# PSUM's eight banks dealt out anew in a fused attention and feed-forward kernel: four for the scores of the exponentials, two for the maxima

## The chip, the cores and the metric

The kernel runs on one core of one Trainium2 chip. The metric is the device time of one execution in microseconds (us). The names of the engines in the rows are those of the profile: PE is TensorE's matmul, PEld its weight load, DVE is VectorE, ACT is ScalarE, POOL is GpSimd, SP is SyncE, which here issues all DMAs.

## The reference

For x of 1024 rows by 512 columns, in fp32:

```
q = x Wq (32 heads of 16)      k, v = x Wkv (8 groups of 16, each shared by 4 heads)
ctx = softmax(causal(q k^T) / 4) v
x1  = layernorm(x + ctx Wo + bo)
out = layernorm(x1 + x1 W^T + bias + LoRA(x1))
```

LoRA(x1) is a low-rank product of 8 adapters of rank 16; the kernel adds it into W beforehand.

## The kernel before, in words

**Units and cycles.** The queries are cut into two halves of 512, and the heads into 8 groups of 4; a half and a group are a *unit* (`NU` = 16, units 8 to 15 are the second half). A unit's scores for the exponentials are worked off in *cycles* (`CYCLES`, 80 of them, numbered 0 to 79): a cycle is 256 of the unit's queries against two blocks of 128 keys. Each cycle has four *pieces* (three where it lies on the causal diagonal); a piece is one matmul of 128 keys by 512 columns (line 1401), and ScalarE turns it into probabilities with one exponential (line 881), 288 in all. Afterwards 16 small matmuls (line 1379, `accumulate`) multiply the cycle's probabilities by v into bank 6.

**Maxima.** The exponentials need each row's maximum beforehand, so each unit's scores are computed a second time, queries on the partitions, some three cycles ahead. This work is cut into 304 *chunks* of at most one PSUM bank (`CHUNKS`): `chunk_scores` on TensorE (line 1164, 1 to 4 matmuls per chunk) and `chunk_max` on VectorE (lines 937 and 944). Of unit 8 on a query block has chunks against the first half's keys (`own` false, one `TENSOR_REDUCE`, line 937) and chunks against its own half (a masked maximum per head, line 944, followed by a short read of the accumulator). A unit's maxima are then split into three bf16 parts by GpSimd (lines 673 to 677), turned by TensorE (line 1172), copied by ScalarE (line 759) and moved by SyncE (line 520) into rows of the unit's queries, so that the score matmul subtracts them.

**Fillers.** Besides, TensorE's order has *fillers*, at most one per cycle (`FILL`): the remaining projections (Q, VT, WE) in cycles 0 to 19, and for each of the first four output blocks the six steps T1a, T1b, T2, WO, T3, FF from cycle 24 on, at offsets 0, 2, 5, 7, 10, 13 in blocks of 14 cycles (24 to 37, 38 to 51, 52 to 65), closer together in the last. Q, WO and FF are long ones (12 matmuls, three after each of the four lots), the others short. The last four output blocks follow after the cycles.

**TensorE's order in a cycle.** It is written out by hand: for each of four lots, the lot's chunks (`chunks_of_cycle`, 0 to 2 chunks), then one piece, then a part of the filler; after the fourth, `accumulate` for the cycle before, then possibly a turn of maxima. Engines take their instructions strictly in this order; VectorE takes the chunks in the same order, with the filler's results between them at fixed places (after T1a or T1b a normalisation of the context at the next cycle's start; after WO and FF the residual there, and the moments after the first lot; after T2, T3 and the projections a subtraction after the first lot).

**Banks.** PSUM has eight banks. Bank 6 holds the products with v. `ST_BANKS` = 3 banks (3 to 5) are dealt in turn to the pieces: a piece waits until the exponential of the piece three before it is done (line 1400). `MAX_BANKS` = 3 banks (0 to 2) and bank 7 (`MISC`) are shared by chunks, fillers and turns. `place_banks` (line 221) deals them out before the program is built: each user takes the bank that has been in use longest, except that a bank given to a filler or a turn is held (`held`) until the end of the next cycle; late fillers, of the last unit's lead, take bank 7. What a chunk has to wait for is in `CHUNK_BEHIND`: the chunk that had its bank before (`was_read`, line 1139, waits until VectorE has read it), or a filler. In this text the *distance* of a chunk is by how many chunks it is behind the one that it waits for. From the 15th chunk on, the distance is 3 for 195 chunks, 4 for 48, 2 for 15; 32 wait for a filler or a turn. The 15 with distance 2 lie in cycles 11, 14, 38 and 52, where two banks are held at once.

```
was_read(CHUNK_BEHIND[n])
for k, j in enumerate(heads):
    last = nc.tensor.matmul(PS[:, CHUNK_BANK[n], k * width:(k + 1) * width], ...)
last.then_inc(max_scores, 1)
```

**Start and end.** The products ahead of the cycles use banks 3 to 6 in a ring of their own (`RING`, `job_bank`); the first 14 chunks lie there, in banks `n % MAX_BANKS`. `FIRST_BEHIND` (line 1347) says which of these products had banks 3 to 6 before the first pieces. From the piece `WIDE` (number 255, in cycle 71) on, when no chunk is left, the pieces rotate over all six banks 0 to 5, whatever the division is.

Of the kernel before, what the change touches and what calls it, by code (L numbers as in the profile page):

```python
# [19 lines left out]
def postln_kernel(nc, x, wq, wkv, wo, bo, lora_a, lora_b, w, bias, lora_w, xt, out):  # L20
# [39 lines left out]
    def key_blocks(cyc):  # L60
        p = CYCLES[cyc][2]
        return 2 * p, 2 * p + 1
# [5 lines left out]
    def pieces(cyc):  # L68

        first = [(0, range(0, 2), 0), (0, range(2, 4), 0)]  # L70
        return first + ([(1, range(0, 4), P)] if on_diagonal(cyc) else [(1, heads, 0) for _, heads, _ in first])
# [66 lines left out]
    def nth(job, kinds):  # L138

        return sum(1 for j in JOBS[:JOB[job] + 1] if j[0] in kinds)  # L140
# [74 lines left out]
        return [lot[len(lot) * q // 4:len(lot) * (q + 1) // 4] for q in range(4)]  # L215


    MAX_BANKS, ST_BANKS = 3, 3
    PV_BANK, MISC = 6, 7

    def place_banks():
# [66 lines left out]
    with ctx:  # L288
# [126 lines left out]
        def score_bank(e):  # L415

            return MAX_BANKS + e % ST_BANKS if e < WIDE else (e - WIDE) % (MAX_BANKS + ST_BANKS)
# [4 lines left out]
        def freed(job):  # L422

            kind, b, _ = job
            if kind == "rows":
                return nm_rows, b + 1
            if kind in ("T1a", "T1b"):
                return ctx_ready, 2 * b + (2 if kind == "T1b" else 1)
            if kind in ("T2", "WO", "T3", "FF"):
                return {"T2": ct_ready, "WO": y1_read, "T3": x1t_ready, "FF": y2_read}[kind], b + 1  # L430
            if kind in BY_ACT:
                return v_read, nth(job, BY_ACT)
            return job_freed, nth(job, DVE_KINDS)
# [704 lines left out]
        def _(pe):  # L1138
# [208 lines left out]
            FIRST_BEHIND = {3 + n % RING: JOBS[n] for n in range(NJOB_A - RING, NJOB_A)}  # L1347
# [37 lines left out]
            def piece_scores(cyc, k):  # L1385

                u, s, _ = CYCLES[cyc]
                i, heads, skip = pieces(cyc)[k]
                kb = key_blocks(cyc)[i]
                e = SCORE_BANKS[cyc] + k  # L1390
                if e < ST_BANKS:
                    pe.wait_ge(*freed(FIRST_BEHIND[score_bank(e)]))
                elif WIDE <= e < WIDE + MAX_BANKS:
                    pe.wait_ge(max_read, len(CHUNKS))
                elif e >= WIDE + MAX_BANKS + ST_BANKS:
                    pe.wait_ge(probs, e - MAX_BANKS - ST_BANKS + 1)
                elif e >= WIDE:
                    pe.wait_ge(probs, WIDE)
                elif e >= ST_BANKS:
                    pe.wait_ge(probs, e - ST_BANKS + 1)  # L1400
                nc.tensor.matmul(PS[:, score_bank(e), :], KS[0:NROW, u % G, kb * P:(kb + 1) * P],  # L1401
                                 QS[0:NROW, u % SLOTS, heads[0]:heads[-1] + 1, s * HQ + skip:(s + 1) * HQ],
                                 start=True, stop=True).then_inc(scores, 1)

            for cyc, (u, _, _) in enumerate(CYCLES):
                if cyc == 0:
                    rows_moved()
                elif cyc == FIRST[u]:
                    pe.wait_ge(nm_in, 16 * NPART * u)
                for j, lot in enumerate(chunks_of_cycle(cyc)):  # L1410
                    for n in lot:
                        chunk_scores(n)
                    if j < len(pieces(cyc)):
                        piece_scores(cyc, j)
                    if cyc == rows_cycle(1) + 1 and j == 0:
                        turn_maxima(1)
                    filler(cyc, j)
                if cyc:
                    accumulate(cyc - 1)
                if cyc in ROWS_AT and ROWS_AT[cyc] > 1:  # L1420
                    turn_maxima(ROWS_AT[cyc])
# [65 lines left out]
```

## Time and profile before

| what | value |
|---|---|
| median of 3 runs | 337.27 us (336.91 to 337.57) |
| the profiled execution | 337.42 us, its span 335.7 us |
| PE, matmul | 320.8 us busy, 2493 instructions |
| PEld, weight loads | 170.9 us |
| DVE | 256.7 us |
| ACT | 217.3 us |
| POOL | 137.7 us |
| granted TensorE clock | 0.997 of full speed |

The span is the time from the first to the last profiled instruction; 1.7 us of the execution lie around it. Times in the rows are from the span's start. Matmuls are pipelined: the time from one's start to its end includes the way through the array, and the next starts before that. How full TensorE is must therefore be read from start to start. The cycles begin at 34.9 us (cycle 0) and end at 301.9 us with the last `accumulate`; the chunks end with cycle 69, at 273 us.

### The profile page before, as it was taken

To read this page: it belongs to the slowest core of one execution; us is meant where nothing else is said; L and a number is where in the kernel's file an instruction comes from. 1 tells how busy PE (TensorE), PEld (TensorE's weight loads), DVE (VectorE), ACT (ScalarE), POOL (GpSimd) and SP (SyncE) were. 2 spreads that over 40 slices of the span, in tenths; PEclk is the share of its full clock that TensorE was granted. 3 is DMA by queue.
4 is the path that set the end of the run, shared out by engine and by line. 5 is a ranking of instruction groups with operands and counts; after the bars stand their busy time and mean duration, and the time that the engine had idled before them with its cause. 6 is when DMAs were issued, how large, how long until landed. Compare 5 with 4: busy or idle time off the path is not lost.

```text
span 335.7 us, 7267 instructions
## 1 busy us (share of the span) xinstructions
PE 320.8 (96%) x2493; PEld 170.9 (51%) x2493; DVE 256.7 (76%) x787; ACT 217.3 (65%) x420; POOL 137.7 (41%) x270
## 2 busy tenths in 40 slices
PE   8999989999999999999999999999999999999992
PEld 3766345455444344454544544544544444558882
DVE  3567968989789989888789889888886961047664
ACT  5563737665757786858667678488584786952431
POOL 8775215464347495347112132212141123331553
PEclk9999999999999999999999999999999999999998
DMA  7687499634235110010020100000000000000002
GB/s 238 251 163 177 127 151 299 204 112 144 63 113 160 49 51 0 3 47 4 8 72 3 49 3 3 0 31 3 3 0 3 32 2 1 2 33 1 2 31 94
DMA packets 15363, 22.96 MB, mean 68 GB/s; under 512 B 3232, under 2 KB 8512, under 8 KB 15328
## 3 DMA queue, kind: packets, MB, share of 16 engines
q1 hardware_dynamic: 15328, 22.51, 23.6%
q8 instruction: 20, 0.33, 0.4%
q14 instruction: 15, 0.12, 0.1%
HBM read 16.29 MB, written 6.03 MB: 66 GB/s over the span
## 4 chain that ended last, share of the span: by engine, by line
PE 74%; DVE 5%; DMA 5%; ACT 4%; issue 4%; POOL 3%; SPq 3%; POOLq 0%; DVEq 0%; ACTq 0%
PE PS L1379 18%; PE PS L1224 17%; PE PS L1164 15%; PE PS L1401 15%; ACT PB L881 3%; DMA scr_q<-parts 2%; PE PS L1305 2%; PE PS L1297 2%; DVE scrap L944 2%; DVE MX L937 2%; PE PS L1239 2%; DMA X<-in_L_attn_x_turned_dram 1%; SPq L498 1%; POOL parts L590 1%; SPq L510 1%
## 5 line engine op out<-in xcount | busy, mean ns | idle before, releaser
L881 ACT ACTIVATE PB<-PS 128x512 f32<-128x512 f32 x288 | 155.5, 604 | 57.9 <-PE PS L1401 56.8
L944 DVE CUSTOM_DVE_ANT_0 scrap<-PS,mask 128x128 bf16<-128x128 f32 (+3 forms) x256 | 111.6, 487 | 15.9 <-PE PS L1164 15.2
L1164 PE MATMUL PS<-KS,QS 96*128 96x512 bf16 (+3 forms) x384 | 108.0, 329 | 2.2 <-DVE MX L937 1.0
L1401 PE MATMUL PS<-QS,KS 99*128 99x512 bf16 x288 | 106.3, 382 | 1.4 <-DMA QS<-NMR 1.1
L937 DVE TENSOR_REDUCE MX<-PS 128x1 f32<-128x512 f32 x128 | 81.9, 684 | 12.6 <-PE PS L1164 11.9
L711 POOL TENSOR_SCALAR_AFFINE_SELECT PB<-PB 128x256 f32<-128x256 f32 (+1 forms) x96 | 46.0, 483 | 102.7 <-ACT PB L881 99.7
L1379 PE MATMUL PS<-PB,VX 128*32 128x256 f32 (+1 forms) x1280 | 78.8, 364 | 0.6 <-ACT PB L881 0.3
L1164 PEld LDWEIGHTS PS<-KS,QS 96*128 96x128 bf16 x384 | 32.9, 97 | 49.7 <-issue 13.3
L1379 PEld LDWEIGHTS PS<-PB,VX 128*32 128x32 f32 x1280 | 33.5, 109 | 40.4 <-issue 17.5
L1401 PEld LDWEIGHTS PS<-QS,KS 99*128 99x128 bf16 x288 | 27.5, 98 | 30.8 <-ACT PB L881 7.4
L1224 PE MATMUL PS<-XT,WQ 128*128 128x512 f32 x120 | 37.4, 434 | 0.4 <-ACT NMR L759 0.4
L1224 PE MATMUL PS<-XT 128*128 128x512 f32 x96 | 28.1, 427 | 0.6 <-DVE MX L937 0.6
L1224 PE MATMUL PS<-WQ,XT 128*128 128x512 f32 x96 | 28.3, 427 | 0.0
L1224 PEld LDWEIGHTS PS<-XT,WQ 128*128 128x128 f32 x120 | 22.0, 190 | 5.9 <-ACT NMR L759 1.3
L692 POOL TENSOR_SCALAR mv<-mv 128x1 f32<-128x1 f32 x15 | 3.4, 227 | 48.7 <-DVE mv L1029 48.6
L944 DVE DVE_READ_ACCUMULATOR2_ANT MX<- 128x1 f32 x256 | 21.2, 83 | 0.0
L1224 PEld LDWEIGHTS PS<-XT 128*128 128x128 f32 x96 | 17.9, 190 | 4.6 <-DVE MX L937 1.1
L1224 PEld LDWEIGHTS PS<-WQ,XT 128*128 128x128 f32 x96 | 17.9, 190 | 4.0
L785 ACT ACTIVATE RAW<-PS 128x256 f32<-128x256 f32 x32 | 12.4, 387 | 10.6 <-PE PS L1379 10.4
L803 ACT ACTIVATE TC<-RAW,shift,rstd 128x512 f32<-128x512 f32 x7 | 5.7, 817 | 13.4 <-POOL shift L694 13.4
L747 ACT ACTIVATE parts<-PS 128x512 bf16<-128x512 f32 x10 | 6.0, 597 | 12.9 <-PE PS L1224 10.2
L590 POOL TENSOR_TENSOR parts<-TC,parts 128x512 bf16<-128x512 f32 x8 | 9.4, 1179 | 6.4 <-DVE NMPS L967 3.3
(102 smaller groups left out, 276.3 us busy)
## 6 DMA issues: line engine op xcount, KB each, us to landing
scr_q<-parts SPq DMA_DIRECT2D x8, 384.0 KB, 4.2
QS<-scr_q SPq DMA_DIRECT2D x15, 192.0 KB, 3.0
X<-in_L_attn_x_turned_dram SPq DMA_DIRECT2D x8, 256.0 KB, 5.8
X<-in_L_attn_x_dram SPq DMA_DIRECT2D x8, 256.0 KB, 2.8
out_dram<-TC SPq DMA_DIRECT2D x8, 256.0 KB, 2.0
QS<-scr_q SPq DMA_DIRECT2D x15, 128.0 KB, 3.0
RAW<-in_L_attn_Wo_dram SPq DMA_DIRECT2D x2, 512.0 KB, 4.9
RAW<-in_L_ffn_W_dram SPq DMA_DIRECT2D x2, 512.0 KB, 4.1
```

The lines of the kernel that those rows point to most:

```text
L590: nc.gpsimd.tensor_tensor(parts[:, s, 2, :], rest[:, s, :], parts[:, s, 1, :], ALU.subtract)\
L711: nc.gpsimd.affine_select(out=blk, in_=blk, compare_op=ALU.is_ge, fill=0.0, base=0, pattern=[[0, len(heads)], [1, P]], channel_multiplier=-1)\
L785: nc.scalar.activation(RAW[:, u, cols], PS[:, PV_BANK, cols], ACT.Copy).then_inc(raw_out, 1)
L881: nc.scalar.activation(PB[:, cyc % NP_BUF, k, :], PS[:, score_bank(e), :], ACT.Exp, scale=SCALE)\
L937: nc.vector.tensor_reduce(part[:, j0:j1, 0:1], bank, AX, ALU.max).then_inc(max_read, 1)
L944: last = nc.vector.tensor_tensor_reduce(out=scrap[:, n % 2, (j - j0) * width:(j - j0 + 1) * width], in0=bank[:, j - j0, :], in1=mask[:, HT ...
L1164: last = nc.tensor.matmul(PS[:, CHUNK_BANK[n], k * width:(k + 1) * width], QS[0:ROWS, u % SLOTS, j, qb * P:(qb + 1) * P], KS[0:ROWS, g, k0 ...
L1224: last = nc.tensor.matmul(bank, lhs(a, c), rhs(b, c), start=(k == 0), stop=(k == len(terms) - 1))
L1239: last = nc.tensor.matmul(job_bank(n), WQ[:, a, c, col:col + P], XT[:, b, c, 0:HT], start=(c == k == 0), stop=(c == NC - 1 and k == 2))
L1297: last = nc.tensor.transpose(bank[:, g * P:(g + 1) * P], RAW[:, h * G + g0 + g, qb * P:(qb + 1) * P], ident[:, :])
L1379: last = nc.tensor.matmul(PS[32 * j:32 * j + 32, PV_BANK, s * HQ + skip:(s + 1) * HQ], VX[:, key_blocks(cyc)[i], u % G, :], PB[:, cyc % NP ...
L1401: nc.tensor.matmul(PS[:, score_bank(e), :], KS[0:NROW, u % G, kb * P:(kb + 1) * P], QS[0:NROW, u % SLOTS, heads[0]:heads[-1] + 1, s * HQ + ...
```

## The change

```diff
-    MAX_BANKS, ST_BANKS = 3, 3
+    MAX_BANKS, ST_BANKS = 2, 4
     PV_BANK, MISC = 6, 7
...
                 e = SCORE_BANKS[cyc] + k
                 if e < ST_BANKS:
-                    pe.wait_ge(*freed(FIRST_BEHIND[score_bank(e)]))
+                    if score_bank(e) in FIRST_BEHIND:
+                        pe.wait_ge(*freed(FIRST_BEHIND[score_bank(e)]))
                 elif WIDE <= e < WIDE + MAX_BANKS:
```

Banks 2 to 5 go to the pieces, in turn, and banks 0, 1 and 7 to chunks, fillers and turns. A piece now waits for the exponential of the piece four before it. The first piece goes to bank 2, which no product of the start had, so that it has nothing to wait for there. `place_banks` deals the chunks and fillers out again by its rule, with one bank less; the order of instructions on every engine stays as it is, and so does their number. Bank 2's last user before piece 0 is one of the first unit's direct query moves, for which the first chunk waits already.

## Rows read from the trace of the kernel before

**Rows 1.** The page: busy time of the engines, and the chain that ended last

```profile
PE 320.8 (96%) x2493; PEld 170.9 (51%) x2493; DVE 256.7 (76%) x787; ACT 217.3 (65%) x420; POOL 137.7 (41%) x270
...
PE 74%; DVE 5%; DMA 5%; ACT 4%; issue 4%; POOL 3%; SPq 3%; POOLq 0%; DVEq 0%; ACTq 0%
```

**Rows 2.** Stretches: length, busy of PE, PEld, DVE, ACT, POOL, clock, DMA, GB/s

```profile
50.00:123.00 73.00, 70.54 (x588) 34.78 (x590) 64.88 (x244) 51.27 (x109) 39.89 (x80) 1.00 0.43 133
123.00:169.00 46.00, 45.98 (x397) 22.39 (x393) 40.20 (x118) 32.36 (x63) 23.63 (x38) 1.00 0.10 26
274.00:302.00 28.00, 27.16 (x256) 13.87 (x257) 5.96 (x15) 21.29 (x43) 8.33 (x19) 1.00 0.03 11
```

**Rows 3.** Timeline of cycle 27: start, length, engine, line; four chunks, distance 3

```profile
133.08 0.39 PE L1164 MATMUL PS<-KS,QS 96*128 96x512 bf16 x1
...
133.50 0.69 DVE L944 CUSTOM_DVE_ANT_0 scrap<-PS,mask 128x512 bf16<-128x512 f32 x1
...
134.12 0.08 DVE L944 DVE_READ_ACCUMULATOR2_ANT MX<- 128x1 f32 x1
...
134.26 0.09 PEld L1164 LDWEIGHTS PS<-KS,QS 96*128 96x128 bf16 x1 [0.20 <-DVE MX L944]
134.40 0.38 PE L1164 MATMUL PS<-KS,QS 96*128 96x512 bf16 x1
...
134.73 0.08 DVE L944 DVE_READ_ACCUMULATOR2_ANT MX<- 128x1 f32 x1
...
134.92 0.86 PE L1379 MATMUL PS<-PB,VX 128*32 128x256 f32 x16
...
135.71 0.39 PE L1164 MATMUL PS<-KS,QS 96*128 96x512 bf16 x1
```

**Rows 4.** Stretches of cycles 38, 52 and 66: same work; columns as before

```profile
169.45:172.83 3.38, 3.04 (x32) 1.48 (x29) 3.21 (x8) 2.23 (x4) 1.07 (x3) 1.00 0.00 0
214.90:218.25 3.35, 3.03 (x32) 1.48 (x29) 3.18 (x8) 2.23 (x4) 1.07 (x3) 1.00 0.00 0
261.15:264.01 2.86, 2.86 (x32) 1.56 (x29) 2.72 (x7) 2.12 (x4) 1.07 (x3) 1.00 0.00 0
```

**Rows 5.** Timeline of cycle 38: its three chunks, the last at distance 2

```profile
170.30 0.38 PE L1164 MATMUL PS<-KS,QS 96*128 96x512 bf16 x1
...
170.53 1.85 DVE L937 TENSOR_REDUCE MX<-PS 128x1 f32<-128x512 f32 x3
...
171.24 0.39 PE L1164 MATMUL PS<-KS,QS 96*128 96x512 bf16 x1 [0.34 <-DVE MX L937]
```

**Rows 6.** Timeline of cycle 66: the same chunks, the last at distance 3

```profile
262.43 0.38 PE L1164 MATMUL PS<-KS,QS 96*128 96x512 bf16 x1
```

**Rows 7.** Timeline of cycle 29: first chunk's end on DVE, third chunk's start on PE

```profile
139.95 0.38 PE L1164 MATMUL PS<-KS,QS 96*128 96x512 bf16 x1
...
140.12 0.08 DVE L944 DVE_READ_ACCUMULATOR2_ANT MX<- 128x1 f32 x1
```

**Rows 8.** Timeline of cycle 36: fourth chunk's start on PE, second chunk's end on DVE

```profile
162.21 0.38 PE L1164 MATMUL PS<-KS,QS 96*128 96x512 bf16 x1
...
162.75 0.08 DVE L944 DVE_READ_ACCUMULATOR2_ANT MX<- 128x1 f32 x1
```

**Rows 9.** Timeline of cycle 11: two chunks in one lot, beside a long filler

```profile
79.69 0.50 PE L1164 MATMUL PS<-KS,QS 96*128 96x384 bf16 x2
...
80.25 0.55 DVE L944 CUSTOM_DVE_ANT_0 scrap<-PS,mask 128x384 bf16<-128x384 f32 x1
...
80.72 0.08 DVE L944 DVE_READ_ACCUMULATOR2_ANT MX<- 128x1 f32 x1
```

**Rows 10.** Waits of pieces' weight loads: us in total, times, longest

```profile
PEld PS L1401 <- ACT PB L881: 7.4, 21, 0.8
```

**Rows 11.** Timeline around 43 us: unit 1's maxima copied, and moved by SyncE

```profile
42.33 0.27 ACT L759 ACTIVATE NMR<-PS 48x128 bf16<-48x128 f32 x1
...
43.87 3.05 SPq L520 DMA_DIRECT2D QS<-NMR  x3
```

## The prediction

> **What bounds the kernel now.** I read the page's busy times and its chain first [rows 1]. VectorE is busy for 76% of the span and matmuls for 96%, but a matmul's row includes the way through the array, so that 96% may hide idle time. The chain that ended last runs over TensorE for 74% of the span. The stretches [rows 2] say where: from 123 to 169 us, matmuls cover 45.98 of 46.00 us, while VectorE has 40.20 and ScalarE 32.36.
>
> How full TensorE is shows start to start in one cycle. Cycle 27 [rows 3] has four chunks of one bank, four pieces and no filler. Its first chunk starts at 133.08, its fourth (after three chunks and three pieces) at 134.40: six matmuls in 1.32 us, 0.22 us each. The fourth chunk and the fourth piece take 0.44 more, to 134.84, and the 16 small matmuls start at 134.92; the next cycle starts at 135.71. Of 2.63 us, 0.08 are not a matmul's own time. The stretches of cycles look like this nearly everywhere from 50 to 274 us: **TensorE's issue is the bound**, and whatever keeps it waiting there lengthens the kernel one for one. There is no cover.
>
> The Trainium skill (Perfetto Trace Analysis, Identifying the Most-Contended Engine) says to judge TensorE's headroom not by matmul busy time but by MFU and by the weight loads' busy share, and the other engines by occupancy. By the weight loads' 51% against VectorE's 76% [rows 1] VectorE would be the most contended engine and a short stop of TensorE could be absorbed: the sum would be near 0. The spacing of 0.22 us decides against that for this kernel; what the rule would give is the first rival.
>
> **What the change removes.** A piece waits for the exponential four before it, no longer three. The present wait shows as 7.4 us of idle weight loads in 21 places [rows 10]. But a load is done ahead while the matmul before it still runs: in cycle 27 one waited 0.20 us and the array had no pause [rows 3]. ScalarE is busy for 32.36 of 46.00 us [rows 2], and `accumulate` waits for all of the previous cycle's exponentials in any case. So this gives between 0 and 7.4 us; I take 0.5, near the lower end, by that load of cycle 27.
>
> After piece 255 nothing changes (six banks in either version), except that piece 257 now waits for the exponentials of the cycle before, which `accumulate` waits for right behind it: below 0.2 us, taken as 0. That is the stretch from 274 us on in which PE is busy for 27.16 of 28.00 us [rows 2]. The first 14 chunks use two banks in turn where they had three; the chain there runs over DMAs, not over them: nothing.
>
> **What it adds.** Going through `place_banks` with two banks plus bank 7, the distance is 2 for 197 chunks, 3 for 46 and 1 for 15 (before: 3 for 195, 4 for 48, 2 for 15). The 15 at distance 1 are those in cycles 11, 14, 38 and 52: one bank left for the chunks, because two are held. TensorE takes instructions in order, so a chunk that waits holds back the piece, the filler and `accumulate` behind it, and with them ScalarE.
>
> Three durations price such a wait [rows 3]. A chunk's first matmul starts at 133.08 and VectorE at 133.50: 0.42 us. VectorE's read takes 0.69; the next one starts 0.62 after it started (134.12). From the end of the reading (134.12 + 0.08 = 134.20) to the weight load of the chunk that waited (134.26) are 0.06 us.
>
> *A natural experiment stands in the trace.* Cycles 38, 52 and 66 have the same matmuls, but the last chunk is at distance 2 in the first two and at distance 3 in the third. They last 3.38, 3.35 and 2.86 us [rows 4]. In cycle 38 that chunk starts at 171.24, with 0.34 us of idle array ahead of it, when the first of three reads (from 170.53, 0.69 long) is done [rows 5]; in cycle 66 it starts at 262.43, while that stretch of reads is still in its first 0.25 us [rows 6]. So a distance of 2 costs 0.5 us in this cycle.
>
> **The price of each kind of cycle** (cycles 3 to 69; 67 of them).
> - *Four or five chunks, short or no filler, the last ones at distance 2: 24 cycles.* In cycle 27 the fourth chunk would wait for the second, whose read ends at 134.73 + 0.08 = 134.81; it would start at 134.86 in place of 134.40: 0.46 us [rows 3]. In cycle 36 (four heads in the second chunk, longer on VectorE) the second ends at 162.83, so the fourth starts at 162.88 in place of 162.21: 0.67 [rows 8]. Where a short filler lies between, its matmuls (0.44 us) cover part of the wait: 0.2 to 0.4. In the first half VectorE is fuller: 0.5. Mean 0.44: **10.5**.
> - *Three chunks at distance 2: 18 cycles.* In cycle 29 the first chunk's read ends at 140.12 + 0.08 = 140.20, the third starts at 140.25 in place of 139.95: 0.30 [rows 7]. Fourteen at 0.3, three after a WO (the moments delay VectorE) at 0.6, one after a FF, cycle 66, at the 0.5 of the natural experiment: **6.5**.
> - *Distances of 3 only: 11 cycles.* The fourth needs the first: 133.08 + 0.42 + 0.69 + 0.06 = 134.25, before the 134.40 at which it starts. 0 to 0.2 each: **0.6**.
> - *Long filler with two chunks in some lots: 8 cycles.* Three filler matmuls of 0.23 us per lot stand between; only 5 and 8 have a remainder, of 0.3: **0.6**. The two 2-chunk cycles, 3 and 12: 0.
> - *Cycles 11 and 14, distance 1.* The second chunk of a lot must wait for the first to be read. In cycle 11 two chunks start at 79.69 and, one matmul later, at 79.85; alone in its bank the second could start after 0.42 + 0.56 + 0.06, that is 1.04 us after the first: 0.9 more [rows 9]. Three such lots in cycle 11 and two in cycle 14, at 0.9 to 0.96, less the 0.4 that TensorE waits there now: **4.3**.
> - *Cycles 38 and 52, distance 1.* First read from 170.53 to 171.22, so the second chunk starts at 171.27 in place of 170.30; its read ends 0.42 + 0.69 later, at 172.38, and the third starts at 172.43 in place of 171.24 [rows 5]: 1.2 each, **2.3**.
>
> Cycles 0 to 2 are not in the list. There the bound is SyncE, which at 43.87 moves unit 1's maxima, after it has issued what is ahead of them; ScalarE had copied them at 42.60 [rows 11]. VectorE reads chunks back to back here, and distance 2 keeps it so (0.06 + 0.42 us from one read's end to a next chunk's start there, against 0.47 from read to read of 384 columns [rows 9] and 0.61 of 512): a delay below 1.27 us is covered, taken as 0. The turns and fillers wait for a bank whose last chunk is two chunks back at least, and with more time between; their DMAs (line 520) are asked for three cycles ahead: 0.
>
> Sum: 10.5 + 6.5 + 0.6 + 0.6 + 4.3 + 2.3 = 24.8, less 0.5, is **24.3 us**. The profiled execution took 337.42, which gives 361.7; the median stands 0.15 below it: **361.5 us**.
>
> **The bounds.** Upwards: taking for each cycle the largest delay that the new distance would cause against VectorE's present times, also where VectorE is behind for another reason, the cycles 3 to 69 come to 26.3 us, and with the series of waits at distance 1 (2.8 more) to 29.1. Some 40 fillers and turns, whose banks are now handed on one chunk earlier, would add 4 at 0.1 each: 33, or 370. Downwards: where a delayed TensorE lets VectorE catch up, the next cycle's wait is shorter. With half the price in the first two kinds (8.5 less) and in the four cycles at distance 1 (3.3 less), 12.5 are left: 350.
>
> **Rivals.**
> 1. *The waits are absorbed and the pieces' fourth bank pays (faster or unchanged).* Were TensorE's idle time hidden in the 96%, the longer waits would fill it, and up to the 7.4 us of [rows 10] would come back: 330 to 337. It decides if ScalarE's exponentials, not VectorE's reads, are what TensorE waits for in the end. Against it: the 0.22 us spacing, 0.08 us of free time in cycle 27, and the 0.5 us of cycles 38 and 52. Chance 0.05.
> 2. *A smaller loss, 338.1 to 350.* VectorE catches up and most cycles lose 0.1 to 0.2 us: 50 cycles by 0.15 are 7.5, and half of the 6.6 for distance 1, together 11: 348. For it: VectorE has 6 us free in each 46 [rows 2]. Against it: the free time is of use only if chunks are there, and two banks hold two of them while `accumulate` takes 0.8 to 1 us. Chance 0.12.
> 3. *Waits add up beyond the sum, over 370.* A late chunk delays unit maxima, these the move by SyncE, and a unit's first piece waits for the DMA (about 3 us); 14 units by 1 us would give 14 more: 375. It decides where the lead of two to three cycles (6 to 9 us) is used up; nothing in the trace is near that. Chance 0.05.
> 4. *The clock.* Every stretch shows a granted clock of 1.00, cycle 38 with its 0.34 us of idle array too [rows 4, 5]. If more such pauses let it fall to 1.2 GHz from 2.4 in one cycle of three of the 224 us between 50 and 274, 75 us would come on top: 436. The Trainium skill (TensorE: Matmul & The Clock Gate, A second HAM failure mode) reports a kernel whose cycling through PSUM banks idled the engine so often that its clock oscillated. The trace shows pauses but no fall. Chance 0.02.
>
> The forecast, 350 to 370, has 0.76. The range is that one, with its lower end at 348 to take in the point of rival 2; it leaves out rivals 1, 3 and 4 and most of 2, about 0.2. A measurement here can tell about 0.2%, 0.7 us, from no change: faster 0.03, same 0.02, slower 0.95.
>
> **What the profile after would show.** The weight loads of line 1164 idle ahead of nearly every cycle's last chunk, put down to VectorE (lines 937 and 944), some 25 us more; cycle 27 takes about 3.1 us; cycle 11 grows by 2.5, cycles 38 and 52 by 1.2, cycle 66 by 0.5; long-filler cycles and everything after 274 us keep their length; busy times of VectorE and ScalarE are unchanged, and ScalarE waits more for line 1401. Wrong would be the sum if cycle 27 kept 2.63 us or if waits for line 881 had carried real time; wrong would be its size if the first chunk of a cycle waited too.

## The result, and the profile after

| | before | after |
|---|---|---|
| median, us | 337.23 (336.91 to 337.57, 4 runs) | 364.03 (363.43 to 364.06, 4 runs) |
| ratio, with its 95% interval | 1 | 1.0785 (1.0771 to 1.0798) |
| span of the profiled execution, us | 335.7 | 362.3 |

The change makes the kernel 26.8 us slower; forecast were 24.3. The page after, busy times and the chain [rows 1], then three groups of instructions (busy us, mean ns of one, idle time before them and what ended most of it):

```profile
span 362.3 us, 7267 instructions
...
PE 331.6 (92%) x2493; PEld 166.7 (46%) x2493; DVE 260.1 (72%) x787; ACT 221.3 (61%) x420; POOL 138.3 (38%) x270
...
PE 62%; DVE 16%; issue 9%; DMA 5%; ACT 3%; SPq 3%; POOL 1%; POOLq 0%; DVEq 0%; ACTq 0%
...
L881 ACT ACTIVATE PB<-PS 128x512 f32<-128x512 f32 x288 | 159.5, 602 | 77.2 <-PE PS L1402 75.3
...
L1164 PE MATMUL PS<-KS,QS 96*128 96x512 bf16 (+3 forms) x384 | 111.0, 330 | 19.9 <-DVE MX L944 12.7
L1402 PE MATMUL PS<-QS,KS 99*128 99x512 bf16 x288 | 106.3, 382 | 0.5 <-DMA QS<-NMR 0.5
```

The same instructions do the same work; the chain has moved from TensorE (74% of the span before) towards VectorE (5% to 16%). The array's idle time ahead of the chunks' matmuls was 2.2 us and is 19.9; ScalarE's ahead of the exponentials grew with it, from 57.9 to 77.2 us, because the pieces stand behind the chunks. (The pieces' line is 1402 now.) The rest of the loss is hidden in this column, since a matmul's row runs on for some 0.16 us after the next could have started (0.38 long, 0.22 apart); the starts show it, below.

Stretches of the kernel before, cut at the starts of cycles 3, 38, 52, 66 and 70, and then those after. A cut lies where the last small matmul of the `accumulate` before has just gone into the array, so that a wait ahead of a cycle's first matmul belongs to that cycle. By such cuts, here and in all that follows, cycle 27 takes 2.74 us in the kernel before and cycle 38 takes 3.48; the prediction counted from first matmul to first matmul, 2.63 and 3.38. Differences between kernels are the same either way.

```profile
48.24:169.43 121.19, 117.64 (x991) 57.50 (x988) 105.92 (x362) 83.79 (x171) 63.52 (x117) 1.00 0.32 95
169.43:214.88 45.45, 45.10 (x387) 21.94 (x384) 39.53 (x111) 32.15 (x62) 10.96 (x27) 1.00 0.05 17
214.88:261.13 46.25, 45.37 (x387) 21.83 (x384) 39.49 (x111) 32.16 (x62) 10.97 (x27) 1.00 0.02 7
261.13:273.27 12.14, 12.01 (x111) 5.82 (x108) 10.95 (x30) 9.54 (x18) 2.53 (x6) 1.00 0.07 24
```

```profile
49.08:184.38 135.30, 123.69 (x991) 55.91 (x988) 107.62 (x362) 85.91 (x171) 63.86 (x117) 1.00 0.28 81
184.38:235.12 50.74, 47.51 (x387) 21.00 (x384) 40.04 (x111) 33.08 (x62) 11.00 (x27) 1.00 0.05 15
235.12:286.68 51.56, 47.76 (x387) 20.89 (x384) 40.02 (x111) 33.08 (x62) 11.00 (x27) 1.00 0.02 7
286.68:300.24 13.56, 12.59 (x111) 5.60 (x108) 11.33 (x31) 9.66 (x18) 2.75 (x7) 1.00 0.06 21
304.25:362.30 58.05, 51.59 (x365) 35.29 (x361) 26.78 (x57) 28.24 (x51) 20.83 (x42) 0.97 0.07 24
```

So +14.1 us in cycles 3 to 37, +5.3 in each of the two blocks of 14 cycles, +1.4 in cycles 66 to 69, +0.8 before cycle 3 and -0.35 in cycles 70 and 71: 26.6, the difference of the spans. From cycle 72 to the end nothing changes (58.07 before; the granted clock of that stretch was 0.98 then). The granted clock is 1.00 in every stretch of chunks.

Most of the 0.8 us before cycle 3 is one wait. The first chunk of cycle 0, at distance 2 now, has to wait until VectorE has read the chunk two before it:

```profile
35.69 0.32 PE L1164 MATMUL PS<-KS,QS 96*128 96x384 bf16 x1 [0.67 <-DVE MX L944]
```

The first piece starts at 35.85 in place of 35.09. The same wait, 0.67 to 0.69 us, stands in the traces of all variants below with two banks, but for the one with half reads, where it is 0.23; in those with three banks or more it is not there.

Cycle 27 [rows 3], after:

```profile
144.63 0.39 PE L1164 MATMUL PS<-KS,QS 96*128 96x512 bf16 x1
...
145.06 0.69 DVE L944 CUSTOM_DVE_ANT_0 scrap<-PS,mask 128x512 bf16<-128x512 f32 x1 [0.21 <-PE PS L1164]
...
145.67 0.08 DVE L944 DVE_READ_ACCUMULATOR2_ANT MX<- 128x1 f32 x1
...
145.81 0.10 PEld L1164 LDWEIGHTS PS<-KS,QS 96*128 96x128 bf16 x1 [0.63 <-DVE MX L944]
...
146.42 0.10 PEld L1164 LDWEIGHTS PS<-KS,QS 96*128 96x128 bf16 x1 [0.50 <-DVE MX L944]
146.42 0.39 PE L1164 MATMUL PS<-KS,QS 96*128 96x512 bf16 x1
```

The third chunk starts 0.06 us after the first was read (145.75), the fourth as long after the second (146.36): 1.79 us after the cycle's start where it was 1.32.

Cycle 38 [rows 5], at distance 1 now, each chunk behind the read of the one before:

```profile
186.19 0.39 PE L1164 MATMUL PS<-KS,QS 96*128 96x512 bf16 x1 [0.78 <-DVE MX L937]
...
186.62 0.69 DVE L937 TENSOR_REDUCE MX<-PS 128x1 f32<-128x512 f32 x1 [0.48 <-PE PS L1164]
...
187.37 0.39 PE L1164 MATMUL PS<-KS,QS 96*128 96x512 bf16 x1 [0.57 <-DVE MX L937]
```

From one chunk to the next 1.18 us: 0.43 through the array, 0.69 of reading, 0.06 back. VectorE itself is idle for 0.48 us in between: at distance 1 both engines wait for each other.

### The profile page after: what moved, and what is told of

Same layout as the page of the kernel before. It is cut to its first block, busy times and chain, and to the rows that moved or that the text cites. A ratio compares the mean times of both kernels' runs of the same rounds, so it can differ in the third digit from the quotient of the medians.

```text
span 362.3 us, 7267 instructions
## 1 busy us (share of the span) xinstructions
PE 331.6 (92%) x2493; PEld 166.7 (46%) x2493; DVE 260.1 (72%) x787; ACT 221.3 (61%) x420; POOL 138.3 (38%) x270
## 4 chain that ended last, share of the span: by engine, by line
PE 62%; DVE 16%; issue 9%; DMA 5%; ACT 3%; SPq 3%; POOL 1%; POOLq 0%; DVEq 0%; ACTq 0%
PE PS L1379 17%; PE PS L1224 15%; PE PS L1164 14%; PE PS L1402 10%; DVE scrap L944 5%; DVE MX L937 4%; ACT PB L881 2%; DMA scr_q<-parts 2%; PE PS L1297 2%; PE PS L1239 1%; PE PS L1305 1%; DVE stats L1027 1%; DMA QS<-NMR 1%; DVE MX L944 1%; DMA X<-in_L_attn_x_turned_dram 1%
## 5 line engine op out<-in xcount | busy, mean ns | idle before, releaser
L881 ACT ACTIVATE PB<-PS 128x512 f32<-128x512 f32 x288 | 159.5, 602 | 77.2 <-PE PS L1402 75.3
L944 DVE CUSTOM_DVE_ANT_0 scrap<-PS,mask 128x128 bf16<-128x128 f32 (+3 forms) x256 | 112.9, 487 | 24.0 <-PE PS L1164 23.5
L1164 PE MATMUL PS<-KS,QS 96*128 96x512 bf16 (+3 forms) x384 | 111.0, 330 | 19.9 <-DVE MX L944 12.7
L937 DVE TENSOR_REDUCE MX<-PS 128x1 f32<-128x512 f32 x128 | 82.4, 684 | 24.5 <-PE PS L1164 24.3
L1402 PEld LDWEIGHTS PS<-QS,KS 99*128 99x128 bf16 x288 | 27.5, 98 | 24.3 <-issue 8.2
L944 DVE DVE_READ_ACCUMULATOR2_ANT MX<- 128x1 f32 x256 | 21.2, 83 | 0.0
```

The costliest lines, as they stand in the source:

```text
L881: nc.scalar.activation(PB[:, cyc % NP_BUF, k, :], PS[:, score_bank(e), :], ACT.Exp, scale=SCALE)\
L937: nc.vector.tensor_reduce(part[:, j0:j1, 0:1], bank, AX, ALU.max).then_inc(max_read, 1)
L944: last = nc.vector.tensor_tensor_reduce(out=scrap[:, n % 2, (j - j0) * width:(j - j0 + 1) * width], in0=bank[:, j - j0, :], in1=mask[:, HT ...
```

## The experiments

**The pieces' bank alone.** The planner as if there were two banks for the maxima, the pieces on three as before:

```diff
-        user = {bank: None for bank in (*range(MAX_BANKS), MISC)}
+        user = {bank: None for bank in (0, 1, MISC)}
...
-            take_chunk(n, n % MAX_BANKS)
+            take_chunk(n, n % 2)
```

> Maxima on banks 0, 1 and 7 as in the changed kernel, pieces on three banks as before; bank 2 lies idle before piece 255. If the loss is the chunks' shorter distance alone: the changed kernel's 364.0 us plus the little that the pieces' fourth bank gave (0.3 to 0.5 us in cycle 70), 364.3 to 364.7. If the fourth bank of the pieces costs or gives something of its own, it lands elsewhere: above 366 if the bank hid waits for the exponentials, below 363 if it did harm.

Measured: 365.01 us (364.55 to 367.58), ratio 1.0844 (1.0800 to 1.0888). Per cycle it is the changed kernel, apart from cycle 70 (2.33 us as before, 1.86 in the changed kernel) and 71 (2.03 against 2.15), and from the start: all of this execution lies 0.6 us later already ahead of cycle 0, of which cycle 3 gives 0.27 back. The fourth bank of the pieces gives 0.35 us in cycles 70 and 71 and nothing that shows elsewhere. The slowest execution, 367.58 us, had a granted clock of 0.947, the others 0.995 or 0.996; the median lies 0.3 us above what I expected. The chunks' idle time is the changed kernel's to a tenth:

```profile
L1164 PE MATMUL PS<-KS,QS 96*128 96x512 bf16 (+3 forms) x384 | 111.0, 330 | 19.9 <-DVE MX L944 12.7
```

**The bank moved the other way.**

```diff
-    MAX_BANKS, ST_BANKS = 3, 3
+    MAX_BANKS, ST_BANKS = 4, 2
...
-            take_chunk(n, n % MAX_BANKS)
+            take_chunk(n, n % 3)
```

> The bank moved the other way: maxima on banks 0 to 3 and 7, pieces on two (4 and 5). By the same arithmetic a piece would wait for the exponential two before it: 0.42 (array) + 0.60 (exponential) + 0.06 = 1.08 us against the 0.88 at which it starts now, so at least 0.2 to 0.3 us per cycle and more where ScalarE has other work, 15 to 22 us over 67 cycles, less about 3 that the chunks of cycles 10 to 20 wait for VectorE now: 349 to 357. If pieces are hidden anyway (ScalarE is the least busy of the three), 334 to 337.

Measured: 348.44 us (348.21 to 349.22), ratio 1.0333 (1.0316 to 1.0350): the mechanism as expected, 0.6 us below the stated size. Cycle 27 takes 3.06 us in place of 2.74, and the waits are now the pieces', for the exponentials (7.4 us in 21 places before [rows 10]):

```profile
PEld PS L1401 <- ACT PB L881: 47.4, 103, 1.2
```

Three and three is the best of the three splits: moving one bank costs 11 us in this direction and 27 in the other.

**One block only.** Bank 2 barred to chunks and fillers in cycles 38 to 51 of the kernel before:

```diff
-                    take_chunk(n, [bank for bank in oldest if bank not in [b for b, _, _ in held]][0])
+                    take_chunk(n, [bank for bank in oldest if bank not in [b for b, _, _ in held]
+                                   and not (bank == 2 and 38 <= cyc < 52)][0])
```

(and the same bar in `take_misc`, left out here).

> The kernel before, but bank 2 is barred to chunks and fillers in cycles 38 to 51 alone. If each cycle's wait is lost on its own: 5.3 us (what these 14 cycles lost in the changed kernel), 342.5, and all other cycles keep their length within 0.1, but for cycle 52, whose chunks are at distance 2 either way. If waits add up over units or shift the others, the loss goes on behind cycle 52 or is less than 4.

Measured: 341.64 us (341.14 to 342.24), ratio 1.0128 (1.0112 to 1.0145). The same four stretches:

```profile
48.29:169.21 120.92, 117.73 (x991) 57.48 (x988) 105.92 (x362) 83.78 (x171) 63.51 (x117) 1.00 0.31 94
169.21:219.93 50.72, 47.51 (x387) 21.00 (x384) 40.00 (x111) 33.07 (x62) 10.96 (x27) 1.00 0.05 15
219.93:265.37 45.44, 45.09 (x387) 21.91 (x384) 39.51 (x111) 32.16 (x62) 10.96 (x27) 1.00 0.02 8
265.37:277.52 12.15, 12.02 (x111) 5.82 (x108) 10.97 (x30) 9.55 (x18) 2.53 (x6) 1.00 0.06 24
```

The barred block lost 5.27 us, as in the changed kernel, and nothing went on behind it: **the losses are local and add up**. The next block is even 0.81 us shorter. That was not expected and has a cause of its own: in cycle 65 of the kernel before, the filler FF must take bank 7 (a late filler), into which the chunk just before it was written. The array's idle time there, in the kernel before (0.56 us in the row; 0.73 from start to start, as the matmul before began at 254.81 and 0.22 us are its own):

```profile
255.76 0.96 PE L1224 MATMUL PS<-XT 128*128 128x512 f32 x3 [0.56 <-DVE MX L937]
```

The barred block happens to shift the banks so that the chunk ahead gets another one; cycle 65 falls from 6.53 to 5.70 us. The last experiment uses that.

**The 16 small matmuls after the second lot.**

```diff
-                if cyc:
-                    accumulate(cyc - 1)
+                    if cyc and j == 1:
+                        accumulate(cyc - 1)
```

> The changed kernel with the whole accumulate (16 small matmuls) after the second lot in place of after the fourth. If a chunk's wait is a matter of how the cycle's matmuls lie between two chunks at distance 2, this only turns the same ring of work: 4 chunks still follow each other with nothing but pieces between, so 4-chunk cycles gain nothing, 3-chunk cycles little: 360 to 365. If it were enough that some long work follows the second chunk, the fourth chunk's wait of 0.43 us in cycle 27 would be covered and most of it come back: 340 to 348.

Measured: 377.29 us (374.09 to 378.13), ratio 1.1167 (1.1117 to 1.1217): slower than both expected. The profiled execution took 374.09 us at a granted clock of 0.997; the three others, 377.12 to 378.13, had 0.986 to 0.988. Its waits, in the array and ahead of weight loads:

```profile
PE PS L1164 <- DVE MX L944: 10.9, 25, 1.0
PE PS L1379 <- ACT RAW L785: 6.8, 13, 0.9
PE PS L1164 <- DVE MX L937: 4.1, 7, 1.0
```

```profile
PEld PS L1379 <- ACT PB L881: 19.3, 31, 1.4
...
PEld PS L1379 <- POOL PB L711: 7.4, 13, 1.2
```

The chunks' waits remain for the most part (15.0 us in the array against 17.3), and new ones came: moved ahead, the small matmuls reach their wait before ScalarE's exponentials, GpSimd's masks and the copy out of bank 6 are done. The place alone is no remedy; how much of the chunks' waits it would have hidden by itself stays open.

**The small matmuls in two halves**, by key block, after the second and the fourth lot, in the changed kernel and in the kernel before:

```diff
-                if cyc:
-                    accumulate(cyc - 1)
+                    if cyc and j % 2:
+                        accumulate(cyc - 1, j // 2)
```

Left out here is the part within `accumulate`: a half passes over the other key block's matmuls, and the first half waits for the first two exponentials of its cycle alone.

> The changed kernel with accumulate cut into two: the half of the cycle's first key block after the second lot, the other half after the fourth. Between two chunks at distance 2 there are then two pieces, one chunk and 0.4 to 0.5 us of small matmuls: 0.88 + 0.5 = 1.4 us against the 1.17 that array, read and signal need. If the wait is that, waits in 3- and 4-chunk cycles vanish (17 to 20 us); the distance-1 waits of cycles 11, 14, 38 and 52 shrink by little: 343 to 348. If the loss is something else (banks, VectorE's throughput), it stays over 358.

> The same cut of accumulate in the kernel before. TensorE has 0.06 us free per cycle there, so nothing to gain but the 3 us of waits in cycles 10 to 20: 334 to 338. If cutting costs something itself (small matmuls of two halves no longer overlap), it shows here: 0.1 us per cycle would be 8 us, 345, and is to be taken off the run above.

Measured: 371.45 us (371.05 to 372.75), ratio 1.1024 (1.0998 to 1.1050), and 355.38 us (354.55 to 355.49), ratio 1.0530 (1.0512 to 1.0547). Both are far above what I expected. By the expectation's words, over 358 would mean that the loss is something else than the distance; but the kernel before shows that the cut costs 18 us by itself. In the kernel before with halves:

```profile
140.92 0.38 PE L1404 MATMUL PS<-QS,KS 99*128 99x512 bf16 x1
...
141.23 0.64 PE L1381 MATMUL PS<-PB,VX 128*32 128x256 f32 x8
...
141.80 0.39 PE L1164 MATMUL PS<-KS,QS 96*128 96x512 bf16 x1
```

A half takes 0.57 us to the next start, and 0.09 pass ahead of it (141.14 to 141.23); twice 0.66 against the whole one's 1.00 + 0.09: 0.23 us per cycle. My expectation named this, with under half of the price. Against each other the two tell what was asked. Cycles 27 and 36 in the changed kernel with halves, then in the kernel before with halves:

```profile
147.66:150.72 3.06, 3.06 (x29) 0.94 (x26) 3.03 (x10) 1.98 (x4) 0.38 (x1) 1.00 0.02 5
178.75:181.94 3.19, 3.19 (x33) 1.08 (x30) 2.85 (x12) 2.48 (x6) 0.00 (x0) 1.00 0.04 8
```

```profile
137.40:140.38 2.98, 2.98 (x29) 1.02 (x26) 2.95 (x10) 1.90 (x4) 0.37 (x1) 1.00 0.03 5
167.53:170.69 3.16, 3.16 (x33) 1.16 (x30) 2.82 (x12) 2.45 (x6) 0.00 (x0) 1.00 0.04 8
```

Cycle 27 loses 0.08 us where it lost 0.48, cycle 36 0.03 where it lost 0.70. With half a microsecond of other work between the second and the third chunk, distance 2 is enough in a cycle of four. It is not where one lot has two chunks (cycle 34: 3.64 to 4.17) or where the moments hold VectorE up (cycle 46: 2.62 to 3.06). In all the distance still costs 16.1 us here (371.45 - 355.38) in place of 26.8; 7.1 of them are in the four cycles at distance 1.

**Half of each chunk read.** The diff, the same in the changed kernel and in the kernel before; the maxima leave out the second half of a chunk's columns, and the exponentials' scale is a hundredth:

```diff
-                    nc.vector.tensor_reduce(part[:, j0:j1, 0:1], bank, AX, ALU.max).then_inc(max_read, 1)
+                    nc.vector.tensor_reduce(part[:, j0:j1, 0:1], bank[:, 0:256], AX, ALU.max).then_inc(max_read, 1)
```

(The masked maximum of line 945 likewise, `width // 2` columns; it and the scale are left out here.)

> The changed kernel, but VectorE reads only the first half of each chunk's columns for the maxima (so half of the scores is left out of them; the exponentials' scale is a hundredth, to keep them finite). A read takes about 0.42 in place of 0.69 us: distance 2 needs 0.42 + 0.42 + 0.06 = 0.90 us against 0.88. If the loss is the reads' duration: 337 to 342, with 2 to 3 us left in the cycles at distance 1. If it is the banks or the waits as such: over 355.

> The kernel before with the same half reads and scale. TensorE bound: 332 to 336, only the waits for VectorE in cycles 10 to 20, 38 and 52 (4 us) go. If VectorE were the bound there, as the most occupied engine, halving its reads (about 65 us of its work) would take off far more: under 325.

Measured: 344.19 us (343.75 to 345.09), ratio 1.0207 (1.0187 to 1.0227), and 333.08 us (332.72 to 334.96), ratio 0.9885 (0.9855 to 0.9915). The line's rows in the changed and in the kernel before, and the second one's busy times:

```profile
L937 DVE TENSOR_REDUCE MX<-PS 128x1 f32<-128x256 f32 x128 | 53.6, 423 | 39.1 <-PE PS L1164 37.6
```

```profile
PE 317.3 (96%) x2493; PEld 171.7 (52%) x2493; DVE 192.7 (58%) x787; ACT 216.5 (65%) x420; POOL 137.3 (41%) x270
...
L937 DVE TENSOR_REDUCE MX<-PS 128x1 f32<-128x256 f32 x128 | 52.7, 422 | 34.7 <-PE PS L1164 34.1
```

In the kernel before, VectorE loses 64 us of work (256.7 to 192.7) and the time falls by 4.4: VectorE, with the highest occupancy, was not what bound it. The Trainium skill (Perfetto Trace Analysis, Identifying the Most-Contended Engine) would have pointed at it, by the weight loads' 51% against VectorE's 76% [rows 1]; the measurement decides. In the changed kernel the same cut takes off 19.8 us: with one bank less, the length of a read has become part of TensorE's path. The remaining loss is 11.1 us in place of 26.8. I had expected less to be left (337 to 342). 5.3 of the 11.1 are in the four cycles at distance 1, for which I had written 2 to 3: a wait there shrinks only by the 0.26 us that the read is shorter, from about 0.9. The rest, which I had put at nothing, is mostly in cycles at distance 2 that my 0.90 against 0.88 us does not describe: 0.64 us in cycle 20, 0.50 in cycles 46 and 60 behind a WO, 0.28 in cycle 36.

**No chunk at distance 1.** In the changed kernel a filler takes the bank of the WE or FF still held:

```diff
-            misc_bank[job] = MISC if late else held[0][0] if held and held[0][2] == "rows" else \
+            misc_bank[job] = MISC if late else held[0][0] if held and held[0][2] in ("rows", "FF", "WE") else \
```

> The changed kernel, but a filler that comes while a WE's or FF's bank is still held takes that bank, so that only one bank is held: no chunk is at distance 1 any more (2 for 218, 3 for 44). If distance 1 costs what the cycles lost beyond distance 2 (1.2 each in cycles 38 and 52, together about 3 to 4 in 11 and 14): 5 to 6 us less than the changed kernel, 358 to 359. If the long fillers there hide most, or the filler's own wait takes its place: 361 to 364.

Measured: 358.87 us (358.77 to 359.39), ratio 1.0633 (1.0610 to 1.0657): 5.2 us less than the changed kernel. Cycles 11 and 38 of it (8.62 and 4.66 us in the changed kernel, 6.04 and 3.48 before):

```profile
80.90:88.28 7.38, 6.12 (x40) 3.32 (x39) 5.06 (x18) 2.77 (x5) 2.29 (x7) 1.00 0.56 149
182.29:185.77 3.48, 3.14 (x32) 1.56 (x29) 3.31 (x8) 2.23 (x4) 1.07 (x3) 1.00 0.00 0
```

Cycles 38 and 52 are back to their length of before, at distance 2 again. In cycle 11 a part remains: the Q filler now waits 1.25 us for the WE before it to be read. That the total meets the expectation is partly luck. The four cycles at distance 1 give 4.4 us (1.24 and 0.75 in cycles 11 and 14, 1.18 and 1.20 in 38 and 52), and 0.81 come from cycle 65, where the edit happens to shift the banks as the barred block did.

**Both edits**, in the changed kernel and in the kernel before.

> The changed kernel with accumulate in two halves and without distance 1. If these two waits are the whole loss: 337 to 340, no slower than the kernel before by more than 1%. If another one is behind them: over 343.

> The kernel before with both edits: distance 3 everywhere in place of 2 in cycles 11, 14, 38 and 52, and accumulate in halves. The 0.5 us each of cycles 38 and 52 and some of the 3 us in cycles 10 to 20 go: 333 to 336. If accumulate in halves costs 0.1 us per cycle, it stays above 340.

Measured: 366.72 us (365.66 to 367.80), ratio 1.0861 (1.0827 to 1.0895), and 357.86 us (357.54 to 358.13), ratio 1.0598 (1.0578 to 1.0617). The halves' 18 us are in both, so neither is near what I expected, and reusing the WE's bank costs the kernel before 2.5 us more (cycle 11: 6.10 to 7.64, cycle 14: 5.98 to 7.28). The difference of the two, 8.9 us, is not simply what the missing bank still costs. In cycles 3 to 69 of the profiled executions it is 6.6 us, and 7.4 without cycle 65, which is 0.81 shorter in the changed kernel only because the banks are shifted. Ahead of cycle 3 it is 3.1 us, and there the granted clock of the changed kernel with both edits fell for about 3 us, from 2.4 to 1.2 GHz:

```profile
45.00:46.00 1.00, 1.00 (x3) 0.61 (x3) 0.00 (x0) 0.00 (x0) 0.07 (x1) 0.50 1.17 125
46.00:47.00 1.00, 1.00 (x5) 0.44 (x4) 0.19 (x1) 0.00 (x0) 0.00 (x0) 0.50 1.20 134
47.00:48.00 1.00, 1.00 (x4) 0.82 (x3) 0.85 (x4) 0.45 (x1) 0.00 (x0) 0.50 1.00 100
```

Before it fell, TensorE had stood still for 0.54 us up to 43.35 and for 0.78 us up to 44.80. The changed kernel has the pause of 0.78 us in the same place, up to 43.44, and kept 1.00; so what made the clock fall here stays open. Two executions of this variant had 0.990 over all and took 367.41 and 367.80 us, the two with 0.997 took 365.66 and 366.04.

**A version that beats both.** The kernel before, with two weak places of the planner mended, the second one by a rule that can do without the luck of the barred block:

```diff
-            late = cyc < 0 or cyc >= FIRST[NU - 1] - 8
-            misc_bank[job] = MISC if late else held[0][0] if held and held[0][2] == "rows" else \
+            late = cyc < 0 or cyc >= FIRST[NU - 1] - 5
+            misc_bank[job] = MISC if late else held[0][0] if held and held[0][2] in ("rows", "FF") else \
```

> The kernel before (three and three, accumulate whole), with two edits of the planner alone: a filler after a FF takes the FF's bank (distance 3 in place of 2 in cycles 38 and 52), and bank 7 is forced on late fillers only from cycle 68 on, not from 65 (in the kernel before, the FF of cycle 65 must take bank 7 right behind the chunk just written there, 0.86 us of idle array). If waits for a bank are lost one for one and locally: 0.4 us each from cycles 38 and 52, 0.8 from cycle 65, up to 0.35 from 69, together 2 us: 335.2 to 335.8. If the time is only handed on to later cycles: 337.

Measured: 335.47 us (334.87 to 336.38), beside 337.21 of the kernel before, ratio 0.9945 (0.9925 to 0.9964). Cycles 38 and 52 take 2.97 us (3.48 and 3.46 before), cycle 65 takes 5.70 (6.53), 69 takes 3.44 (3.75), while 67, where two chunks are now at distance 2, takes 3.31 (3.01), and 39 and 53 take 0.08 more each: 1.7 us less, and all of it arrives at the end. It is a gain of 0.5%, small but clear of the noise by its interval.

## Why the prediction was right, point by point

- **What bounds the kernel: right.** TensorE's issue, read start to start. With a quarter of VectorE's work gone the kernel before gains 1.2%; and each wait put in shows at the end in full (one block: 5.27 us in the block, none given back behind it).
- **The price of a distance: right in mechanism and size** for plain cycles. 0.42 of array, a read, 0.06 back. Cycle 27 forecast 0.46, measured 0.48; cycle 36, 0.67 and 0.70; cycle 29, 0.30 and 0.32; cycle 66, 0.5 and 0.52; cycle 38, 1.2 and 1.18; cycle 11, 2.5 and 2.58.
- **The sum by kinds**, forecast and measured: short-filler cycles of four or five chunks 10.5 and 11.0; three chunks 6.5 and 7.3; distance 3 only 0.6 and 1.0; long fillers 0.6 and 0.2; cycles 11 and 14 4.3 and 4.65; 38 and 52 2.3 and 2.4; cycles 3 and 12 0 and -0.5. Together 24.8 and 26.1. Two sizes were too low: of the three-chunk cycles, 35, 49 and 63, behind a T3, lost 0.47 and not 0.3, because T3's subtraction on VectorE stands between; and cycle 20, behind a WE, lost 1.1 where a mean of 0.5 stood for the first half.
- **The start and cycles 0 to 2: put at nothing, and half wrong.** The prediction has VectorE reading back to back there, so that distance 2 would cost nothing. Ahead of cycle 0 it does not: in the changed kernel VectorE copies queries from 33.42 to 34.73 (line 1094), reads the chunk that went into the array at 31.68 only after that, from 34.76 to 35.54, and the first chunk of cycle 0, which needs that bank, waits 0.67 us. The first piece comes 0.76 us later, the first `accumulate` 0.9, and the maxima of unit 1 are copied at 43.39 in place of 42.60 [rows 11]. SyncE's move itself was not held up, as forecast, so the first piece of cycle 3 waits 0.53 us for it in place of 1.06: of 0.84 us, 0.53 are covered and 0.31 are not. The prediction's sign that its size would be wrong, a first chunk of a cycle that waits, came true in this one cycle.
- **The gain of the pieces' bank: 0.5 forecast, 0.35 measured**, all of it in cycles 70 and 71. The size was picked from a range of 0 to 7.4 us by one weight load of cycle 27, and the place was not foreseen; that it came so close is partly luck.
- **The other signs.** The weight loads of line 1164 wait 62.1 us for VectorE in place of 21.2 (lines 944 and 937 together): 41 more where I wrote some 25, since a load's wait counts also where the matmul before it still runs. The busy times of VectorE and ScalarE were to stay the same and rose by 3.4 and 4.0 us. The instructions did not get longer (an exponential 602 ns on the average, 604 before); busy time counts rows that overlap once (288 exponentials of 604 ns would be 174 us, and the page before has 155.5), and fewer overlap when they stand apart.
- **Rivals.** Absorbed waits: excluded by the result, and by the barred block, whose waits arrived at the end in full. A smaller loss by VectorE's catching up: no such thing in any cycle of the steady blocks. Waits that add up: excluded by the barred block. The clock: 1.00 in all stretches of chunks despite pauses up to 0.88 us, and 0.995 to 0.999 in the four executions of the changed kernel; the oscillation of which the Trainium skill tells (TensorE: Matmul & The Clock Gate, A second HAM failure mode) does not occur in it. Among its variants the clock did fall in some executions, as told above: once seen in a trace, for about 3 us, and down to 0.947 of full speed over a whole execution. So the chance of 0.02 was for a real thing, at a much smaller size than the 75 us.

## What to carry to other kernels

Count buffers by the time between two users, not by the number of engines: a bank that comes round after two chunks must cover array, read and signal (0.42 + 0.69 + 0.06 = 1.17 us here) with the work between (0.88), and what is missing is lost each time that such a pair comes up, if the engine that waits is the one at its limit. Such a price can be read from the old trace: take each user's start and set it against the end of the read that it will have to wait for. The Trainium skill (Perfetto Trace Analysis, Optimization Strategy) says that the same gap repeating on the engine that should be saturated can mean too little PSUM; the gaps of 0.3 to 0.7 us in most cycles after the change are of that kind. In the kernel before, two such places of the planner (a filler forced on the bank just written, two banks held at once) were worth 0.5% of the time.

## What the runs showed of the hardware that was not expected

Cutting a run of 16 small fp32 matmuls as the profile counts them (two rows for each matmul of the code; 32 columns of weights each, over four parts of the array) into two runs of eight makes each half take 0.57 us in place of 0.50, and each entry into such a run costs 0.09 us more: 0.23 us per cut, 18 us over the kernel. Why a half takes more than half was not tried.

TensorE's waits for a PSUM bank that VectorE had yet to read, up to 0.88 us long and in most cycles of about 3 us, left its granted clock at 1.00 from 50 to 300 us in the changed kernel. That is no rule for all such kernels: in the changed kernel with both edits the clock fell to 1.2 GHz from about 45 to 48 us.
